# A two-layer graph-attention kernel on one core: a new order of work on every engine, and the weight set-up moved into the first steps

## The reference

```
# layer 0
q, k = x @ Wq + bq, x @ Wk + bk                 # 8 heads of 32
attn = softmax(q k^T / sqrt(32))
out  = sum over r in 0..3 of (attn * (adj == r)) @ (x @ Wv[r] + bv[r])
x    = LN(x + out @ Wo + bo) * g1 + beta1
x    = LN(x + gelu(x @ W1 + b1) @ W2 + b2) * g2 + beta2
# layer 1
e    = leaky_relu(q k^T, 0.2), masked where adj <= 0
h    = LN(softmax(e) @ v) * g1 + b1
out  = LN(concat(h, x) @ Wffn^T) * g2 + b2 + x
```

## Time and profile before

| what | us |
|---|---|
| median of 3 runs (2405.45 to 2411.77) | 2407.12 |
| the profiled execution | 2403.04 |
| its span, first to last instruction | 2401.2 |
| TensorE matmuls busy | 2284.4 (95%) |
| VectorE busy | 2115.4 (88%) |
| ScalarE busy | 2120.3 (88%) |
| GpSimd busy | 1698.0 (71%) |

### The profile page before, as it was taken

How to read it: one execution, slowest core, us unless ns; L and a number is a source line. 1 busy time by engine, 2 the same in 40 slices (tenths; PEclk the granted TensorE clock), 3 DMA queues, 4 the chain that set the end, 5 groups by cost and what they waited for, 6 DMA issues and landing times.

```text
span 2401.2 us, 80726 instructions
## 1 busy us (share of the span) xinstructions
PE 2284.4 (95%) x30284; PEld 1850.1 (77%) x30284; DVE 2115.4 (88%) x3987; ACT 2120.3 (88%) x5976; POOL 1698.0 (71%) x1870
## 2 busy tenths in 40 slices
PE   2799999999999999999999999999999999999984
PEld 1577888788788788788788887877877877877863
DVE  3779999999999999999999999999999998998973
ACT  4689999998999999999899999999999999999973
POOL 1467777777777777777777777777777777777763
PEclk9999999999999999999999999999999999999997
DMA  4447557657667666756756765766665675675553
GB/s 132 87 89 141 106 115 137 113 110 133 115 112 130 121 111 124 129 110 117 138 107 115 138 114 109 133 120 106 130 125 107 124 132 109 115 142 103 108 99 67
DMA packets 948549, 280.53 MB, mean 117 GB/s; under 512 B 877249, under 2 KB 947393, under 8 KB 948161
## 3 DMA queue, kind: packets, MB, share of 16 engines
q1 hardware_dynamic: 944992, 271.95, 61.0%
q10 hardware_dynamic: 3168, 3.41, 0.5%
HBM read 40.38 MB, written 16.78 MB: 24 GB/s over the span
## 4 chain that ended last, share of the span: by engine, by line
PE 56%; ACT 6%; DMA 6%; SPq 3%; issue 3%; DVE 2%; POOL 1%; DVEq 0%; ACTq 0%; POOLq 0%
PE bank L523 43%; PE bank L621 6%; PE bank L584 4%; DMA pT<-p1h 3%; ACT bank L778 3%; DMA xT<-x_rows 2%; PE bank L602 1%; SPq L477 1%; SPq L470 1%; ACT p0h L849 1%; ACT p L767 1%; SPq L427 1%; POOL x_rows L1178 1%; PE bank L554 1%; PE bank L569 1%
## 5 line engine op out<-in xcount | busy, mean ns | idle before, releaser
L973 DVE TENSOR_TENSOR pm<-pT,bank 128x4096 f16<-128x4096 f16 x256 | 573.4, 2277 | 9.8 <-DMA pT<-p0h 9.4
L523 PE MATMUL bank<-wv,xT 128*128 128x512 f16 (+1 forms) x2304 | 449.6, 345 | 0.0
L778 ACT ACTIVATE bank<-bank,p_nmax 128x128 f32<-128x128 f32 x1024 | 355.8, 369 | 23.9 <-DVE p_nmax L959 19.4
L1178 POOL TENSOR_TENSOR h<-h_f,h 128x512 f16<-128x512 f32 x256 | 292.6, 1164 | 96.6 <-ACT h L754 96.5
L523 PEld LDWEIGHTS bank<-wv,xT 128*128 128x128 f16 x2304 | 220.8, 98 | 178.3 <-issue 18.2
L523 PE MATMUL bank<-yT,w 128*128 128x256 f16 x3072 | 356.7, 273 | 0.3 <-DMA yT<-x_rows 0.2
L523 PE MATMUL bank<-w,h 128*128 128x256 f16 x3072 | 345.7, 272 | 2.7 <-POOL h L1178 2.7
L1178 POOL TENSOR_TENSOR x_rows<-x,x_rows 128x512 f16<-128x512 f32 x128 | 148.2, 1157 | 270.2 <-ACT x_rows L821 157.6
L767 ACT ACTIVATE p<-p,p_nmax 128x128 f32<-128x128 f32 x1024 | 336.5, 435 | 0.8
L523 PEld LDWEIGHTS bank<-yT,w 128*128 128x128 f16 x3072 | 295.3, 98 | 41.8 <-issue 0.8
L523 PEld LDWEIGHTS bank<-w,h 128*128 128x128 f16 x3072 | 295.9, 98 | 36.2 <-issue 2.8
(11 more groups left out here) (125 smaller groups left out, 4888.6 us busy)
## 6 DMA issues: line engine op xcount, KB each, us to landing
x_sb<-in_x_dram SPq DMA_DIRECT2D x64, 256.0 KB, 3.0
adj_i<-in_adj_dram SPq DMA_DIRECT2D x128, 128.0 KB, 2.7
out_dram<-x2b SPq DMA_DIRECT2D x64, 256.0 KB, 3.0
xT<-x_rows SPq DMA_TRANSPOSE x128, 3.2
pT<-p0h SPq DMA_TRANSPOSE x128, 4.6
oT<-o_rows SPq DMA_TRANSPOSE x128, 3.2
pT<-p1h SPq DMA_TRANSPOSE x128, 5.0
pm<-in_L_gnn_W_dram ACTq DMA_DIRECT2D x1, 1024.0 KB, 13.1
```

The source lines that it names most:

```text
L523: last = nc.tensor.matmul(o, l, r, start=(first and k == 0), stop=(final and k == len(todo) - 1))
L778: last = nc.scalar.activation(ps(f"s0_{r}")[:, at:at + P], ps(f"s0_{r}")[:, at:at + P], ACT.Exp, bias=p0_nmax[:, r, g, c:c + 1], accum_out ...
L973: V_.tensor_tensor(pm0[g][:, s], pT0[g][:, s].unsqueeze(1).broadcast_to([P, REL, HEADS, P]), edges[:, g].unsqueeze(2).broadcast_to([P, REL ...
L1178: return V_.tensor_tensor(to, source, high, ALU.subtract)
```

## The change

Three things change together.

The set-up loses its own block. SyncE loads the first x at once, and issues 35 transfers ahead of its pipeline (22 before), ScalarE 5. The first four weights are split by ScalarE and VectorE right behind the first x. The five later ones (`w1`, `w2`, `wq1`, `wk1`, `wv1`) are copied by ScalarE behind the last probabilities of block 0, and their low parts are now made by GpSimd, behind `x_low(1)`. `Wffn` is no longer turned over by TensorE: GpSimd scales and splits it (`fold_gain`, behind the edge types of block 0), and SyncE turns it over with a transposing transfer.

The order within `steps`, the lags and the bank table are new on all engines. Small tiles are merged (the variance is now overwritten by its own reciprocal root), which changes no amount of work.

SyncE, ahead of its pipeline:

```diff
+                rows_from_x(0)
+                load_weight(sp, "wk0")
+                types_from_adj(0)
+                for r in range(REL):
+                    sp.dma_start(staged["wv0"][:, :, r * D:(r + 1) * D], a["L0_gnn_Wv"][r].rearrange("(k p) n -> p k n", p=P)
+                                 ).then_inc(landed_w["wv0"], 16)
+                sp.wait_ge(S["xT0_lo"], 1)
+                transpose_rows(xT0, x_rows, S["xT0_in"])
+                sp.wait_ge(s_const, CONSTANTS)
+                sp.wait_ge(s_bv_hi, 1)
+                sp.wait_ge(s_bv_lo, 1)
+                for i in range(ROWS):
+                    cols = slice(i % 2 * BANK, (i % 2 + 1) * BANK)
+                    sp.dma_start(bv_rows[i * DH:i * DH + 1, :], bv_hi[:, cols]).then_inc(s_bias, 16)
+                    sp.dma_start(bv_rows[i * DH + 1:i * DH + 2, :], bv_lo[:, cols]).then_inc(s_bias, 16)
+                load_weight(sp, "wo0")
+                load_weight(sp, "wffn")
+                sp.dma_start(b1_row1, row(a["L1_gnn_b1"])).then_inc(s_ends, 16)
+                sp.dma_start(g1_row1, row(a["L1_gnn_g1"])).then_inc(s_ends, 16)
+                rows_from_x(1)
+                for name in ("w1", "w2", "wq1", "wk1", "wv1"):
+                    load_weight(sp, name)
+                for tile, v in late_rows:
+                    sp.dma_start(tile[:], row(a[v])).then_inc(s_rows, 16)
+                sp.wait_ge(s_fold, 4)
+                sp.dma_start_transpose(wffn[:].rearrange("p s c (o j) -> p (s c o) j", o=KC),
+                                       ffn_rows.rearrange("p s c o j -> p (s c o j)")).then_inc(s_wffn, 16)
                 pipeline(steps)
```

GpSimd:

```diff
+                def fold_gain():
+                    pool.wait_ge(landed_w["wffn"], count_w["wffn"])
+                    pool.wait_ge(s_ends, 32)
+                    gained = staged["wffn"][:, :, 0:D]
+                    V_.tensor_tensor(staged["shifted"], gained, b1_row1.unsqueeze(1).broadcast_to([P, KC, D]), ALU.mult).then_inc(s_fold, 1)
+                    V_.tensor_tensor(gained, gained, g1_row1.unsqueeze(1).broadcast_to([P, KC, D]), ALU.mult).then_inc(s_fold, 1)
+                    pool.wait_ge(s_fold, 2)
+                    by_column = staged["wffn"].rearrange("p o (c j) -> p c o j", j=P)
+                    V_.tensor_copy(ffn_rows[:, 0], by_column).then_inc(s_fold, 1)
+                    pool.wait_ge(s_fold, 3)
+                    low(ffn_rows[:, 1], by_column, ffn_rows[:, 0]).then_inc(s_fold, 1)
+
+                def later_weights_low():
+                    for n, (name, tile) in enumerate(later_parts):
+                        pool.wait_ge(s_hi1, n + 1)
+                        low(tile[:, 1], staged[name], tile[:, 0]).then_inc(s_lo1, 1)
...
+                    if m == 0:
+                        fold_gain()
...
+                    if m == 1:
+                        later_weights_low()
...
+                    if m == 0:
+                        pool.wait_ge(s_rows, ALL_ROWS)
```

ScalarE, behind the last probabilities of block 0, and the banks of PSUM:

```diff
+                def later_weights_high():
+                    for name, tile in later_parts:
+                        act.wait_ge(landed_w[name], count_w[name])
+                        nc.scalar.activation(tile[:, 0], staged[name], copy).then_inc(s_hi1, 1)
...
+                    if m == 0 and r == ROWS - 1:
+                        later_weights_high()
...
-    ("v0_0", 1, 1, "v0_lo", 4, 1),
...
+    ("v0_0", 6, 1, "v0_lo", 4, 1),
```

More of the change, by code:

```diff
@@ L164, in build @@
         h = sb("h", [2, FC, T], F16)
-        x2 = [sb(f"x2_{u}", [G, D]) for u in range(2)]
+        x2 = [sb(f"x2_{u}", [G, D]) for u in range(X2R)]
         v1 = sb("v1", [2, G, HEADS, DH + 1], F16)
@@ new lines, in build @@
+        ffn_rows = h_flat[:, 0:4 * KC * KC * P].rearrange("p (s c o j) -> p s c o j", s=2, c=2 * KC, o=KC)
+        shift_rows = h_flat[:, 4 * KC * KC * P:4 * KC * KC * P + D]
+        shift_cols = x2b[:, 0, 0:KC]
+        first_parts = [("wq0", wq0), ("wk0", wk0), ("wv0", wv0), ("wo0", wo0)]
+        later_parts = [("w1", w1), ("w2", w2), ("wq1", wq1), ("wk1", wk1), ("wv1", wv1)]
+        landed_w = {n: ctx.enter_context(nc.semaphore(n + "_landed")) for n in staged if n != "shifted"}
+        count_w = {n: 16 * (REL if n == "wv0" else 1) for n in landed_w}
@@ L649, in queries_keys_1 @@
                     x2_transposed(m)
+                    if m == 0:
+                        pe.wait_ge(s_lo1, 3 if job == "q1" else 4)
                     for c in range(KC):
@@ L1045, in scaled_added @@
                     for g in range(G):
-                        last = V_.scalar_tensor_tensor(to[:, g], rows_in(name, g), rs[:, g:g + 1], added(g), ALU.mult, ALU.add)
+                        last = V_.scalar_tensor_tensor(to[:, g], rows_in(name, g), mv[:, g, 1:2], added(g), ALU.mult, ALU.add)
                     return last
```

632 lines of the change are left out of this document (313 added, 319 removed).

## The result

| | before | after |
|---|---|---|
| median (5 runs each) | 2410.94 | 2399.46 |
| lowest to highest | 2405.45 to 2416.90 | 2396.22 to 2400.36 |
| profiled execution, its span | 2403.04, 2401.2 | 2400.30, 2398.5 |

The ratio is 0.9951, with a 95% interval of 0.9932 to 0.9969: the medians are 11.5 us apart, where 2409 and "the same" were forecast. A second comparison gave 0.9950 (0.9937 to 0.9963). The time lies inside the forecast range of 2391 to 2425, but the kernel did become faster by 0.5%, and no gain was forecast: 2409 is 2 us above the 2407.12 that the forecast started from.

The account below looks back on a forecast made before the run. TensorE was taken as the bound, 35.20 us per steady step, leaving 22.4 us above that floor, besides start and emptying. 2403.04 + 6 - 3 - 1 = 2405.0, with 4.1 for the median 2409; range 2391 to 2425.

Parts of the forecast that it names:

- Start: Set-up to scores(1): scores(0) 21 us earlier, but first probabilities held behind GpSimd's work and Wffn; 6 us loss.
- Steady steps: The filled pipeline's 57 steps: fewer waits for probabilities against a new wait of the queries; -6 + 3 = -3 us.
- -6 for the probabilities: Steady steps: second-layer probabilities leave 0.6 to 0.7 us earlier, so some 6 of 7.7 us of waits go.
- 0 for the other transfer: Steady steps: 7.0 us of waits for the rows for the second layer's queries stay, their place on SyncE unchanged.
- +3 for the queries: Steady steps: queries wait for VectorE's fourth low part with zero slack; 0.05 us per step, 3 us.
- Everything else that moved lands within a few tenths, under TensorE's cover: Steady steps: the other moved instructions, such as the hidden layer's copies, cost or save nothing that shows.
- Emptying: End of the pipeline: GpSimd's low part of the hidden layer comes about 1 us earlier; -1 us.
- The 4.1 us from the profiled execution to the median: Whole kernel: the median lies 4.1 us above the profiled execution's 2403.04, added at the end of the sum.
- steady waits vanish: Rival, steady steps: both late transfers are covered, the 22.4 us go, median 2390, half gives 2401; chance 0.19.
- The bound on VectorE: Rival, steady steps: VectorE's chain to the fourth low part overruns, 0.3 us per step, median 2426; chance 0.22.
- the steady period: Sign: 35.4 to 35.6 us per step expected; under 35.3 or above 35.7 would show the forecast wrong.
- The locked port pair: Rival, start: GpSimd and VectorE hold each other up, 6 us more, 2415; chance 0.08 with late rows at 43.

Follow-up runs that it names:

- a_start1: Changed kernel, GpSimd's first steps reordered: low part of x(1), edge types, folded gain, then bias adds, then the later weights' five low parts; 2372.43 us.
- a_adj1_back: Changed kernel with the load of the second layer's edge types put back behind the transpose of x1; 2407.98 us, ratio 1.0002 to the kernel before.
- a_xt3: Changed kernel with three buffers instead of two for x2's transposed rows; 2392.65 us, ratio 0.9941 to the kernel before.

## Why the prediction was wrong, by its steps

- **Start: right in its chain.** Forecast and measured: scores(0) at 27 and 27.26; rows landed at 39 and 36.97; GpSimd's work 24.5 and 23.4; first probabilities at 66 and 63.46; scores(1) +6 and +4.6 (+5.1 over three traces). The low parts of 2048 columns took 4.08, not 4.5. The gain of 21 us was turned into a loss, as said; a_start1 shows that the position of one addition, which waits for the last row, and of five low parts on GpSimd did it. The ramp behind scores(1) had no term and cost 2.3 in this pair of traces, 1.2 over three.
- **Steady steps: here the sum failed.** It had -6 for the probabilities, 0 for the other transfer and +3 for the queries, -3 in all. Measured -14.4, and -16.2 over three traces. The step had the right place and the wrong sizes. The term for the probabilities was mis-sized: 6 was taken from the 7.7 us of wait rows, but the 12 periods with such a wait lay 10.5 us above 35.20 (each wait breaks an overlap of 0.16 besides), and all of it went. The +3 did not come at all. And "the 7.0 us of the other transfer stay" joined two transfers: 4.3 us were for x's rows, not for the second layer's. Their periods fell from 6.1 to 5.0, those for x2 from 3.2 to 2.5, and all the rest of the 22.4 from 2.7 to 0.4. "Everything else that moved lands within a few tenths, under TensorE's cover" put at nothing what the order brings: without the moved load it still takes 7 to 8 us off the steady stretch (a_adj1_back). Through which transfers it does so can be read in the table of periods; which of the moved instructions does it was not tried one by one.
- **Two misses partly cancelled.** Against the forecast of +6 - 3 - 1 for the trace, the start was off by -1.4, the steady steps by -11.4, the ramp by +2.3 and the emptying by +5.8. That the time fell inside the range owes something to this.
- **Queries against VectorE: the +3 was nothing.** The four low parts took 2.48, as forecast (4 x 0.62). But I left x1 at its old place in the period, and it moved 0.33 us forward with the rest; 0.56 us of slack remained where I had zero. (The 2218.65 of that sum should have been 2218.59 + 0.1 = 2218.69 by its own terms, which changes nothing.)
- **Emptying: -1 forecast, +4.8 measured.** GpSimd's wait did shrink (2.68 to 1.9). What I didn't see is that the last and the feed-forward product now share bank 3. In a steady step the values and the output projection of later blocks lie between them; at the end they don't, and the one waits 4.14 us for the reading out of the other. But of the 4.8 us 4.1 are busy time, 93.75 against 89.64 for the same 1072 matmuls: in the stretches with a granted clock of 0.50, which is 1.2 GHz, TensorE was busy for 24.6 us against 16.1 before, and 8.5 us at half the clock are 4.2 us more than at the full one. That the wait causes this isn't shown: a_start1 and a_xt3 have it too and empty in 131.4 and 129.7. The ramp is alike: 2.6 us more busy time for the same 2066 matmuls at 0.96 instead of 0.98.
- **The 4.1 us from the profiled execution to the median: wrong for the changed kernel.** I carried it over from before. The first profiled execution of after lay above its median. Without it the forecast would have been 2405.
- **The rival "steady waits vanish" was the nearest**: with its -22 (2390) it went too far by 8, its halved form gives 2401, and it had 0.19. The bound on VectorE (2426) did not occur. Of the signs named, the steady period came out at 35.34 us, under the 35.4 to 35.6 and just above the 35.3 that was to prove the forecast wrong.
- **The locked port pair.** GpSimd's 512-column low parts took 1163 ns in the mean in the changed kernel, beside a VectorE that is busy 92% of the steady stretch (1849.88 of 2014.35), and 1.15 to 1.16 at the start:

```profile
L1200 POOL TENSOR_TENSOR p1h<-p,p1h 128x512 f16<-128x512 f32 x256 | 291.9, 1163 | 10.3 <-ACT p1h L796 7.4
```

The rule of the Trainium skill (SBUF — State Buffer, Who interferes with whom) is for VectorE instructions with two SBUF inputs. VectorE's longest groups here read one of their two inputs from a bank of PSUM (`pm<-pT,bank`, `v<-bank,v`), so these rows, like the earlier trace rows, are no test of it, and the 6 us of the rival rested on a condition that they don't show.

## What to carry to other kernels

Where one queue issues a chain of transfers without gaps, look at what stands first in it and at the spread of its issue times, not at the transfer that is waited for last: a load that nobody waits for (0.6 us) cost 8 to 12 us here, and a low part made 1.2 us later 27. Where a profile leaves buffer numbers out, split a wait by its place in the period before giving it to one transfer, and count what a period with the wait lasts, not only the wait. An order that a whole pipeline shares is valued as a whole: half of this one made the kernel 14 to 17% slower. In a start, follow the engine that works while the others wait, and put ahead on it what the next block needs; one addition and five low parts that stood first there held up the second block by 26 us.
